# Where the last pass of a graph kernel loads its block numbers

## The reference, cut to what matters

```python
hi = h[src]; hj = h[dst]
e = leaky_relu(concat([hi, hj]) @ w, 0.2) @ a
exp_e = exp(e)
denom = segment_sum(exp_e, src)
att = exp_e / denom[src]
out = segment_sum(hi * att, dst)
```

## Time and profile before

| what | value |
|---|---|
| median of 3 timed runs | 9324.56 us (9323.96 to 9327.27) |
| the profiled execution, first to last instruction (span) | 10761.6 us |
| last pass in it, first to last weights of a group (L1829) | 9627.4 to 10707.6 us |
| DVE busy over the span | 3994.5 us (37%) |
| POOL busy over the span | 6943.5 us (65%) |
| mean granted clock of PE | 0.672 |

### The profile page before, as it was taken

How to read it: one execution, slowest core, us unless ns; L and a number is a source line. 1 busy time by engine, 2 the same in 40 slices (tenths; PEclk the granted TensorE clock), 3 DMA queues, 4 the chain that set the end, 5 groups by cost and what they waited for, 6 DMA issues and landing times.

```text
span 10761.6 us, 137184 instructions
## 1 busy us (share of the span) xinstructions
PE 4749.1 (44%) x27323; PEld 4216.7 (39%) x27324; DVE 3994.5 (37%) x13681; ACT 3909.3 (36%) x11178; POOL 6943.5 (65%) x7392
## 2 busy tenths in 40 slices
PE   3323222343322323342333332256666666667776
PEld 2222222232222222232222222256666666666665
DVE  2222222222222222222222222256556655568888
ACT  3333333333333333333333333322222222237777
POOL 5666666656666666656666666646666666658886
PEclk6555555566555555565555555677778777789998
DMA  3111111122111111121111111145555555544444
GB/s 81 45 46 45 45 46 45 46 59 51 45 45 46 45 46 46 45 65 47 46 45 46 45 46 45 46 139 149 146 147 148 148 147 147 146 132 138 138 139 133
DMA packets 918236, 875.96 MB, mean 81 GB/s; under 512 B 253109, under 2 KB 764001, under 8 KB 918175
## 3 DMA queue, kind: packets, MB, share of 16 engines
q0 software_dynamic: 239728, 516.96, 18.5%
q1 hardware_dynamic: 614765, 259.14, 8.7%
q10 hardware_dynamic: 63698, 99.36, 3.3%
HBM read 734.15 MB, written 137.96 MB: 81 GB/s over the span
## 4 chain that ended last, share of the span: by engine, by line
issue 26%; another core or an unknown queue 23%; DVE 20%; DVEq 17%; PE 11%; ACT 2%; DMA 0%; ACTq 0%; POOL 0%; SPq 0%; POOLq 0%
DVE agg L1585 8%; DVEq L1562 7%; DVEq L468 5%; DVE agg L1571 4%; PE psum L1251 4%; PE psum L1276 2%; DVEq L1580 2%; PE psum L1270 2%; DVE big L1818 2%; DVEq L1593 1%; DVE work L1692 1%; DVE work L1699 1%; PE psum L1178 1%; DVE work L1689 1%
## 5 line engine op out<-in xcount | busy, mean ns | idle before, releaser
L1178 PE MATMUL psum<-work,rows 128*128 128x128 f32 (+1 forms) x9408 | 2056.2, 394 | 4728.1 <-DVE agg L1585 2465.2
L766 POOL DMA_INDIRECT rows<-table_g,idx_now x3136 | 2966.9, 946 | 1688.0 <-issue 1061.4
L1178 PEld LDWEIGHTS psum<-work,rows 128*128 128x128 f32 x9408 | 1825.5, 284 | 4959.6 <-issue 2822.9
L1585 DVE TENSOR_TENSOR agg<-agg,psum 128x128 f32 x4704 | 1351.4, 287 | 5323.6 <-remote 3145.3
L933 ACT ACTIVATE work<-big,one_col 128x512 f32<-128x512 f32 x1176 | 817.9, 710 | 3315.9 <-remote 2837.2
L766 POOL DMA_INDIRECT rows<-in_x,idx_now x1568 | 1483.3, 946 | 799.3 <-issue 467.6
L923 ACT ACTIVATE big<-iota_w,rel_now 128x128 f32<-128x128 f32 (+1 forms) x4704 | 1501.6, 396 | 429.5 <-remote 345.0
L766 POOL DMA_INDIRECT rows<-table_p,idx_now x784 | 764.3, 975 | 480.8 <-SPq L599 254.9
L1010 ACT ACTIVATE work<-psum 128x256 f32<-128x256 f32 x784 | 295.2, 387 | 1864.9 <-remote 1129.9
L1251 PE MATMUL psum<-work 128*128 128x98 f32 x3168 | 624.3, 362 | 689.0 <-DVE work L1692 362.4
L1251 PEld LDWEIGHTS psum<-work 128*128 128x128 f32 x3168 | 569.5, 269 | 741.3 <-DVE work L1692 392.9
(11 more groups left out here) (211 smaller groups left out, 5718.4 us busy)
## 6 DMA issues: line engine op xcount, KB each, us to landing
rows<-x_of SPq DMA_DIRECT2D x415, 256.0 KB
rows<-table_g,idx_now POOLq DMA_INDIRECT x3136
work<-rel_rows ACTq DMA_DIRECT2D x196, 256.0 KB
x_of<-rows SPq DMA_DIRECT2D x196, 256.0 KB
big<-lo_rows ACTq DMA_DIRECT2D x208, 192.0 KB
x_of<-work SPq DMA_DIRECT2D x147, 256.0 KB
rows<-in_x,idx_now POOLq DMA_INDIRECT x1568
idx_now<-src_t SPq DMA_DIRECT2D x784, 4.0 KB
```

The costliest lines, as they stand in the source:

```text
L766: pool.indirect_dma_start(out=to, out_offset=None, in_=table, in_offset=bass.IndirectOffsetOnAxis(ap=idx_now[:, at:at + 1], axis=0)) \
L1178: ins = pe.matmul(sums_at(q, t % QUAD)[:, 0:wide], ring[:, t, :], span_hot[q][:, t % QUAD, 0:wide], start=True, stop=True)
L1585: dve.tensor_tensor(to, to, sums_at(q, j)[:, 0:P], ALU.add).then_inc(added[j], 1)
```

## The change

The load of eight window numbers is taken out of `weights_of`, where it stood behind the picks and in front of the weights. `add_half` now loads them itself, by two loads of four: one in front of the first addition, one in front of the third. The diff, cut to its core:

```diff
@@ weights_of
                 given = exp_rel_4[:, :, :, ds(TPI + group * HALF, HALF)]
                 dve.lower_ap(given)
-                windows = load_windows(added_next * HALF, DVE_E) if added_next is not None else None
                 dve.wait_ge(hot_act, len(HOT_ACT) * (group + 1))
...
-                return windows
-
-            def add_half(turn, h, windows):
+
+            def add_half(turn, h):
                 group = 2 * turn + h
+                later = None
                 for j in range(HALF):
+                    if j == 0:
+                        windows = load_windows(group * HALF + j, DVE_E, QUAD)
+                    if j == QUAD - 2:
+                        later = load_windows(group * HALF + QUAD, DVE_E, QUAD)
+                    if j == QUAD:
+                        windows = windows + later
                     add_tile(group * HALF + j, windows[j], ps[j // 2][:, (j % 2) * D:(j % 2 + 1) * D],
                              0 if j % QUAD else QUAD)
...
                 for h in range(2):
-                    windows = weights_of(1 - h, 2 * i + h + 1, i + h, 2 * i + h)
+                    weights_of(1 - h, 2 * i + h + 1, i + h)
                     hot_lo(1 - h, i + 1 + h)
-                    add_half(i, h, windows)
+                    add_half(i, h)
...
             for h in range(2):
-                add_half(TURNS - 1, h, load_windows((GROUPS - 2 + h) * HALF, DVE_E))
+                add_half(TURNS - 1, h)
```

More of the change, by code:

```diff
@@ L1811, in hot_lo, with weights_of @@
                                   ALU.is_equal).then_inc(lo_hot_ready, 1)
-            def weights_of(s, group, lap, added_next=None):
+            def weights_of(s, group, lap):
                 dve.wait_ge(looked_up, group + 1)
@@ L1846, in _ @@
                 for h in range(2):
-                    windows = weights_of(1 - h, 2 * i + h + 1, i + h, 2 * i + h)
+                    weights_of(1 - h, 2 * i + h + 1, i + h)
                     hot_lo(1 - h, i + 1 + h)
-                    add_half(i, h, windows)
+                    add_half(i, h)
                 own.leave(TURNS - 2)
-            windows = weights_of(1, GROUPS - 3, TURNS - 2, GROUPS - 4)
+            weights_of(1, GROUPS - 3, TURNS - 2)
             hot_lo(1, TURNS - 1)
-            add_half(TURNS - 2, 0, windows)
-            windows = weights_of(0, GROUPS - 2, TURNS - 1, GROUPS - 3)
-            add_half(TURNS - 2, 1, windows)
+            add_half(TURNS - 2, 0)
+            weights_of(0, GROUPS - 2, TURNS - 1)
+            add_half(TURNS - 2, 1)
             weights_of(1, GROUPS - 1, TURNS - 1)
             for h in range(2):
-                add_half(TURNS - 1, h, load_windows((GROUPS - 2 + h) * HALF, DVE_E))
+                add_half(TURNS - 1, h)
             dve.wait_ge(bank_free, HALF + T)
```

## The result

The change makes the kernel a little slower: 9354.5 us (median of 6 runs, 9351.2 to 9356.7) against 9324.5 us (6 runs, 9323.2 to 9327.3). The ratio is 1.0030, with a 95% interval of 1.0020 to 1.0039. The sign and the place were as forecast; the size was not: 30 us instead of 58.

A forecast was written before the change was run, and what follows sets the result against it. DVE with its sequencer was taken to bound the last pass: 1.66 us paid against 1.11 gained a turn, 56 us over 102 turns, plus 1.5 outside the loop, gave 9324.6 + 58 = 9382 us; range 9345 to 9425 us.

The forecast's parts named there:

- The sign and the place: Slower, in the last pass: 0.55 us lost a turn, 56 us in the loop's 102 turns; slower was given 80%.
- What bounds the pass: Last pass: DVE sets the pace at 5.22 us a group, through datapath and sequencer; POOL's own work is 4.80 us.
- The gain: In front of the weights: with the load gone, the gaps of 0.67 and 0.52 us shrink, gaining 1.11 us a turn.
- How much of a load is hidden: Between DVE's additions: the first load shows 0.46 us, the second 0.37, as the sequencer runs only one instruction ahead.
- rival 4: DVE's loads hide behind datapath work, showing under 0.28 us each on average: 23 us faster, 9301 us; chance 7%.
- The price of a load of four: Each load of four window numbers on DVE: 0.43 us, on a straight line between 0.31 for one and 0.60 for eight.
- Rival 2: Loads between DVE's additions: four numbers cost as one, 0.31 us; 7 us slower in all, 9332 us; chance 12%.
- Rival 3: DVE's sequencer runs ahead of waiting additions, making the third 0.22 us late, not 0.37: 27 us slower, 9352 us; chance 5%.
- The carry-over to the timed runs: The last pass's 58 us apply unscaled to the timed runs; scaled by 0.87 it would be 50 us and 9375.
- floor of about 600 ns: Stated price of a load on DVE: four would cost as much as eight; the prediction found one number at half that.

The follow-up runs named there:

- e5: The kernel before with the eight window numbers loaded once in front of the last pass's loop, none inside it (sums wrong); 9249.8 us, ratio 0.9918.
- e0: The kernel before, unedited, profiled again; span 9323.9 us, last pass 1080.6 us.
- e4: The kernel before with 20 loads of various counts and places behind the last addition, each number used by small copies; four numbers from place 0 took 0.349 us.
- e8: The changed kernel with one load of eight before the first addition, picks behind additions four to seven, two behind the eighth; 9259.1 us, 0.9924 of the kernel before.
- e6: The changed kernel with six picks moved behind additions three to eight, the second load behind the first pick; 9306.6 us, 0.9976 of the kernel before.

## Why the prediction was right and wrong

**What bounds the pass: right.** DVE with its sequencer set the pace, and the pace of POOL, worked out as 4.80 us a group, is close to where e5 stopped (4.83).

**The gain: right to 0.01 us.** Forecast 0.63 and 0.48 us; the gaps went from 0.67 and 0.52 to 0.04 each. No other wait stood behind the load: in the whole pass the weights wait for something else 3 times, 2.3 us.

**How much of a load is hidden: right but for some hundredths.** With the measured 0.345 us in place of 0.43, 0.085 less, the forecast gives 0.375 in front of the first addition (measured 0.83 - 0.46 = 0.37 and 0.86 - 0.46 = 0.40) and 0.285 in front of the third (measured 0.61 - 0.32 = 0.29). Their mean is 0.34 us for each of the four loads of a turn, and rival 4 had worked out that the change wins only under 0.28: that is why it lost. That the sequencer goes no further than a waiting addition is confirmed twice: the second load starts only once the second addition has started and shows in every group of the changed kernel, and with a pick behind each addition the hold is gone (0.44 us a pair).

**The price of a load of four: the term that was mis-sized.** "A straight line between them gives 0.31 + 3/7 x 0.29 = 0.43 us, and I take that" was the failing step. It was 0.345. Four such loads stand in a turn: 4 x 0.085 x 102 = 35 us, and 58 - 35 = 23 us would have been the forecast for a pass that grew by 24.8. Rival 2 had the better price, four numbers for that of one, 0.31 us: the measured one is 0.035 above it and 0.085 under the forecast's. The 12% it had were too few: with two points, one of them a single number, a line had no more behind it than a step. The whole range took the load at 0.35 us or more, and its low end was also stretched for rival 3, so that 9354.5 us lies in it says little for the price.

**Rival 3, a sequencer that runs ahead: right in time, wrong in mechanism.** Its 9352 us are closer to the measured 9354.5 than the forecast's 9382, and that is chance. It let the second load start 0.24 us after the first addition, at 8730.14 in the turn shown; the load starts at 8730.3, after the second addition at 8730.22. With 0.345 in place of 0.43 us it would make the third addition 0.22 - 0.085 = 0.135 us late, where 0.29 were measured.

**The carry-over to the timed runs: right for the pass** (e0). The timed difference of 30 us is some 5 us more than the pass grew. The interval of 19 to 36 us holds both; what the 5 us are is not shown.

**Two stated prices beside the rows.** The rows of e4 give 0.313 us for one number and 0.21 to 0.23 us for each further single one. The Trainium skill's floor of about 600 ns for a `tensor_load` (DMA: Bandwidth & Descriptors, section "Latency and other measured facts"), weighed in the prediction, does not hold for these loads from SBUF. The Trainium skill (Runtime: NRT & Kernel Launch, section "Instruction fetch mechanics") has about 200 ns per register for a `TENSOR_LOAD` from HBM, even in bulk. The trace agrees with that size for single numbers, though they come from SBUF, and not for aligned fours, 0.25 us for four registers. An estimate by that figure would be 0.8 us for four numbers.

## What to carry to other kernels

The table that a load of registers reads should be read in whole fours that start at a multiple of four: four numbers cost little more than one, three cost twice as much, and one place off costs 0.97 us instead of 0.35 (e4, on VectorE's sequencer and a table in SBUF). A load is hidden only where the sequencer is ahead; where each instruction waits for the one before it, the sequencer goes no further, and most of a load shows (0.29 of 0.345 us here). Such chains are loosened by putting independent work of the same engine between their links, which gave here 70 us where moving the load around lost 8 to 44.

## What the runs showed of the hardware that was not expected

The cost of a register load by count and place (e4) is above. In e5 to e8 the test of low parts, the same instruction on the same shape, is sometimes slower: up to 678 ns instead of 420. In e6 its mean is 534 ns, where the earlier trace rows show 0.42 us:

```profile
L1810 DVE TENSOR_SCALAR big<-big,node_c 128x768 bf16<-128x768 int16 x198 | 105.8, 534 | 0.0
```

The traces say what it coincides with. In e5 to e8 together 282 of the 832 tests take over 440 ns, and all but four of these run while POOL is in one of its indirect fetches (L836). In the turn of e6 from 8700 on, the first test stands beside a fetch and the second does not:

```profile
8701.12 0.95 POOL L836 DMA_INDIRECT big<-table_r,idx_now  x1 [0.31 <-issue]
8701.59 0.66 DVE L1810 TENSOR_SCALAR big<-big,node_c 128x768 bf16<-128x768 int16 x1
...
8707.75 0.42 DVE L1810 TENSOR_SCALAR big<-big,node_c 128x768 bf16<-128x768 int16 x1
```

Running beside a fetch is not enough: in e0 some hundred tests start 0.75 us or more after the start of a fetch, most of them while it still runs, and take 420 ns. No run moves the fetch alone, so the cause is argued and not shown. In e6 it cost nothing: the first addition starts 0.72 us after the slow test (8702.31) and 0.74 us after the quick one (8708.49), because the load stands in front of it.
